# MetaFormer block: the clip finished on ScalarE and its sum with x moved from VectorE to GpSimd

## The reference

```python
x = x + conv_ref(ln_c(x), weight, gamma, beta)     # ln_c: normalise over the 64 channels
t = to_tokens(x)                                   # (32, 3136, 64)
t = t + ffn_ref(ln_t(t), ...)                      # ln_t: normalise over the 64 channels again

def conv_ref(x, weight, gamma, beta):
    y = conv3x3(sign(x), sign(weight - mean) * power_of_two)
    yn = (y - mean(y)) * rsqrt(var(y) + 1e-5) * gamma + beta   # statistics over all images and pixels
    return clip(yn, -1.0, 1.0)

def ffn_ref(x, Wr, br, W1, ..., Wo, bo):           # 8 experts, 64 -> 64 -> 64 -> 64
    w = softmax(mean(x, axis=0) @ Wr + br)         # a gate for each pixel, from the mean over the images
    h = relu(bn1(x @ W1 + b1)); h = relu(bn2(h @ W2 + b2))
    return sum over experts of w * (h @ Wo + bo)
```

## Time and profile before

| What | Value |
|---|---|
| Median of 3 runs | 1450.95 us (1448.56 to 1454.09) |
| Profiled execution | 1453.43 us, its span 1451.5 us |
| TensorE (PE) busy | 1362.0 us, 94% |
| VectorE (DVE) busy | 978.6 us, 67% |
| ScalarE (ACT) busy | 882.1 us, 61% |
| GpSimd (POOL) busy | 556.3 us, 38% |
| Mean granted TensorE clock | 0.983 of full speed |

### The profile page before, as it was taken

How to read it: one execution, slowest core, us unless ns; L and a number is a source line. 1 busy time by engine, 2 the same in 40 slices (tenths; PEclk the granted TensorE clock), 3 DMA queues, 4 the chain that set the end, 5 groups by cost and what they waited for, 6 DMA issues and landing times.

```text
span 1451.5 us, 34080 instructions
## 1 busy us (share of the span) xinstructions
PE 1362.0 (94%) x12984; PEld 661.1 (46%) x12984; DVE 978.6 (67%) x1660; ACT 882.1 (61%) x1279; POOL 556.3 (38%) x474
## 2 busy tenths in 40 slices
PE   3999974999999999999999999999999999999998
PEld 2666641444444444354444444444544444344444
DVE  5888871666667766666666666676666667666665
ACT  3666663666666666666666666666666666666643
POOL 7000052433444443344344344444334434434441
PEclk9999985999999999999999999999999999999999
DMA  9999920333233333323333323333323333332221
GB/s 160 171 159 140 132 51 26 66 71 78 46 65 70 66 72 72 64 51 68 65 72 72 78 47 65 66 70 65 78 48 65 69 65 72 72 77 46 53 46 33
DMA packets 361597, 107.08 MB, mean 74 GB/s; under 512 B 353552, under 2 KB 353776, under 8 KB 361456
## 3 DMA queue, kind: packets, MB, share of 16 engines
q1 hardware_dynamic: 360192, 103.49, 38.4%
q0 software_dynamic: 1264, 1.61, 0.6%
HBM read 78.97 MB, written 26.09 MB: 72 GB/s over the span
## 4 chain that ended last, share of the span: by engine, by line
PE 48%; issue 1%; DVE 1%; POOL 0%; ACT 0%; POOLq 0%; ACTq 0%
PE ps L549 15%; PE ps L571 15%; PE ps L587 14%; PE ps L605 2%; PE ps L638 1%; PE ps L613 1%; DVE placed L985 1%; ACT wT L776 0%; PE ps L625 0%; POOL feat L443 0%; POOL feat L446 0%; DVE o L941 0%; PE ps L632 0%; POOLq L257 0%; PE ps L642 0%
## 5 line engine op out<-in xcount | busy, mean ns | idle before, releaser
L931 DVE SCALAR_TENSOR_TENSOR v<-ps,negb,wb 128x448 f32<-128x448 f32 x896 | 570.4, 677 | 297.7 <-PE ps L571 233.8
L740 ACT ACTIVATE h<-ps,bias 128x896 f32<-128x896 f32 x448 | 451.4, 1008 | 349.8 <-PE ps L549 349.8
L549 PE MATMUL ps<-xc,w 64*64 64x448 f32 x3584 | 463.4, 541 | 14.0 <-POOL xc L434 11.0
L571 PE MATMUL ps<-h,w 64*64 64x448 f32 x3584 | 458.4, 539 | 7.4 <-issue 5.1
L587 PE MATMUL ps<-v,wo 64*64 64x448 f32 x3584 | 461.8, 542 | 3.2 <-issue 2.4
L571 PEld LDWEIGHTS ps<-h,w 64*64 64x64 f32 x3584 | 174.2, 133 | 189.0 <-issue 171.9
L549 PEld LDWEIGHTS ps<-xc,w 64*64 64x64 f32 x3584 | 163.4, 132 | 186.4 <-issue 178.9
L464 POOL TENSOR_TENSOR o<-o,upper 128x448 f32<-128x448 f32 x112 | 127.6, 1139 | 305.0 <-DVE o L941 305.0
L587 PEld LDWEIGHTS ps<-v,wo 64*64 64x64 f32 x3584 | 163.4, 133 | 174.8 <-issue 162.9
L456 POOL TENSOR_TENSOR o<-xin,gconst 128x448 f32<-128x448 f32 x112 | 129.8, 1181 | 249.3 <-ACT gconst L781 155.4
L434 POOL TENSOR_TENSOR xc<-xc,spread 128x896 f32<-128x896 f32 x56 | 122.6, 2208 | 166.4 <-DMA spread<-rs_rows 166.3
(11 more groups left out here) (151 smaller groups left out, 840.5 us busy)
## 6 DMA issues: line engine op xcount, KB each, us to landing
xa<-in_x SPq DMA_DIRECT2D x64, 392.0 KB, 6.4
xin<-in_x SPq DMA_DIRECT2D x112, 224.0 KB, 4.1
spread<-rs_rows SPq DMA_DIRECT2D x112, 224.0 KB, 4.2
out<-o SPq DMA_DIRECT2D x224, 112.0 KB, 2.5
rs_rows<-rs SPq DMA_DIRECT2D x112, 3.5 KB
rows<-in_L_ffn_g POOLq DMA_DIRECT2D x2, 256.0 KB, 6.2
rows<-in_L_ffn_v POOLq DMA_DIRECT2D x2, 256.0 KB, 6.8
cwt<-in_L_conv_weight SPq DMA_DIRECT2D x2, 144.0 KB, 2.6
```

The lines of the kernel that those rows point to most:

```text
L549: last = mm(ps[64 * two:64 * two + 64, L1_BANKS + ab, 0:NG], w1[half, P * q + C * two:P * q + C * two + C], xc[half, s, g // 2, ab ^ (g % ...
L571: last = mm(ps[64 * i:64 * i + 64, L2_BANKS[ab] + low, 0:NG], w2[rows_, Q + QUADS * i, :], h[rows_, u % 2, i, ab, :], start=True, stop=True)
L740: A(h[:, u % 2, i], ps[:, L1_BANKS:L1_BANKS + 2, 0:NG], ACT.Relu, bias=bias[:, 0, q:q + 1]).then_inc(h_done[i], 1)
L931: last = V.scalar_tensor_tensor(out=v[:, u % 2, ab, d, :].rearrange("p (b w) -> p b w", w=W), in0=ps[:, L2_BANKS[ab] + d, 0:NG].rearrange( ...
```

## The change

The second half of the clip leaves VectorE. With t = relu(SCALE * y + OFFSET1) as before, ScalarE makes a second pass over the same buffer, t = relu(2 - t), which is 2 - min(t, 2). GpSimd then forms xin - t, which is x + clip(yn) - 1, so `gconst` has a bias of +1. The first pass is now at places 6, 8, 10, 12 and the second (`over`) at 8, 10, 12, 14, ahead of the first pass of that place. The sums have no place of their own: they stand in GpSimd's queue, those of groups 0 and 1 of chunk k + 2 ahead of `norm(k+1)`, those of groups 2 and 3 behind `feature(k+1)`. `add_upper(k, 1)` moves from behind `feature` to ahead of it. Before the chunks, GpSimd forms all four sums of chunk 0 first and those of chunk 1 between `norm(0)` and `feature(0)`.

```diff
-        bn = sb("bn", [P, 17], F32)
+        bn = sb("bn", [P, 18], F32)
+        (TWO = bn[:, 17:18], set to 2.0 by V.memset)
...
         STEADY = Schedule(
-            t=(8, 10, 12, 14), x1=(13, 16, 17, 21), centre=(20, 28),
+            t=(6, 8, 10, 12), over=(8, 10, 12, 14), centre=(20, 28),
...
# GpSimd
+                def add_clip(q, s, g):
+                    if g % 2 == 0:
+                        pool.wait_ge(x_loaded[g // 2], 32 * q + 32)
+                    pool.wait_ge(t_done, G * q + g + 1)
+                    xg = xin[:, s, BG * g:BG * g + BG, :]
+                    nc.gpsimd.tensor_tensor(xg, xg, t[:, g].rearrange("p (b w) -> p b w", w=W), ALU.subtract).then_inc(x1_done, 1)
...
                     add_const(k, s, G - 1)
                     add_upper(k, 0)
+                    if left > 1:
+                        for g in range(2):
+                            add_clip(k + 2, s, g)
                     if left:
                         for p in range(STEPS):
                             norm(k + 1, 1 - s, p)
+                    add_upper(k, 1)
+                    if left:
                         feature(k + 1, 1 - s)
-                    add_upper(k, 1)
+                    if left > 1:
+                        for g in range(2, G):
+                            add_clip(k + 2, s, g)
                     add_upper(k, 2)
...
+                for g in range(G):
+                    add_clip(0, 0, g)
                 for p in range(STEPS):
                     norm(0, 0, p)
+                for g in range(G):
+                    add_clip(1, 1, g)
                 feature(0, 0)
...
# ScalarE
+                def rest_of_clip(q, g):
+                    act.wait_ge(t_low, G * q + g + 1)
+                    A(t[:, g], t[:, g], ACT.Relu, bias=TWO, scale=-1.0).then_inc(t_done, 1)
...
+                    for g in places_at(at.over, h) if at is STEADY else ():
+                        rest_of_clip(q, g)
                     for g in places_at(at.t, h):
                         act.wait_ge(x1_done, G * q + g + 1)
...
-                        A(..., yq, ACT.Relu, bias=OFFSET1, scale=SCALE).then_inc(t_done, 1)
+                        A(..., yq, ACT.Relu, bias=OFFSET1, scale=SCALE).then_inc(t_low, 1)
+                    for g in places_at(at.over, h) if at is AHEAD else ():
+                        rest_of_clip(q, g)
...
-                        A(gconst[:, s, :], ps[:, Y, 0:W], ACT.Copy, bias=-1.0).then_inc(g_done, 1)
+                        A(gconst[:, s, :], ps[:, Y, 0:W], ACT.Copy, bias=1.0).then_inc(g_done, 1)
...
# VectorE
-                    for g in places_at(at.x1, h):
-                        if g % 2 == 0:
-                            dve.wait_ge(x_loaded[g // 2], 32 * q + 32)
-                        dve.wait_ge(t_done, G * q + g + 1)
-                        xg = xin[:, s, BG * g:BG * g + BG, :]
-                        V.scalar_tensor_tensor(out=xg, in0=t[:, g].rearrange("p (b w) -> p b w", w=W), scalar=2.0, in1=xg,
-                                               op0=ALU.min, op1=ALU.add).then_inc(x1_done, 1)
```

More of the change, by code:

```diff
@@ L37, with __init__ @@
 class Schedule:
-    def __init__(self, t, x1, centre, var, root, square, inv, logits, gate, turn, wb):
-        self.t, self.x1, self.centre = t, x1, centre
+    def __init__(self, t, over, centre, var, root, square, inv, logits, gate, turn, wb):
+        self.t, self.over, self.centre = t, over, centre
         self.var, self.root, self.square, self.inv = var, root, square, inv
@@ L81, in metaformer_kernel @@
         wT = sb("wT", [C, W], F32)
-        bn = sb("bn", [P, 17], F32)
-        SCALE, OFFSET, SW, OFFSET1 = bn[:, 0:1], bn[:, 1:2], bn[:, 2:3], bn[:, 16:17]
+        bn = sb("bn", [P, 18], F32)
+        SCALE, OFFSET, SW, OFFSET1, TWO = bn[:, 0:1], bn[:, 1:2], bn[:, 2:3], bn[:, 16:17], bn[:, 17:18]
         gb = sb("gb", [P, 2], F32)
@@ L158, in metaformer_kernel @@
         x_loaded = [sem(f"x_loaded{p}") for p in range(STEPS)]
+        t_low = sem("t_low")
         t_done = sem("t_done")
@@ L217, in metaformer_kernel @@
         STEADY = Schedule(
-            t=(8, 10, 12, 14), x1=(13, 16, 17, 21), centre=(20, 28),
+            t=(6, 8, 10, 12), over=(8, 10, 12, 14), centre=(20, 28),
             var=34, root=36, square=38, inv=(40, 41), logits=58, gate=60, turn=62, wb=63)
         AHEAD = Schedule(
-            t=(0, 0, 0, 0), x1=(0, 0, 0, 0), centre=(1, 2),
+            t=(0, 0, 0, 0), over=(0, 0, 0, 0), centre=(1, 2),
             var=3, root=3, square=3, inv=(3, 3), logits=5, gate=5, turn=5, wb=5)
@@ L337, in _ @@
             def _(pool):
-                for s, n in (*((u, 1) for u in u_done), (feat_done, 1)):
+                for s, n in (*((u, 1) for u in u_done), (feat_done, 1), (x1_done, G)):
                     pool.sem_inc(s, n)
@@ L761, in prep @@
                             y[:, bass.ds(q, 1), BG * g:BG * g + BG, :].rearrange("p o b w -> p (o b) w")
-                        A(t[:, g].rearrange("p (b w) -> p b w", w=W), yq, ACT.Relu, bias=OFFSET1, scale=SCALE).then_inc(t_done, 1)
+                        A(t[:, g].rearrange("p (b w) -> p b w", w=W), yq, ACT.Relu, bias=OFFSET1, scale=SCALE).then_inc(t_low, 1)
+                    for g in places_at(at.over, h) if at is AHEAD else ():
+                        rest_of_clip(q, g)
                     if h == at.var:
@@ L810, in _ @@
                 V = nc.vector
-                for s, n in ((v_done[0], 1), (v_done[1], 1), (out_done, 1), (x1_done, G)):
+                for s, n in ((v_done[0], 1), (v_done[1], 1), (out_done, 1)):
                     dve.sem_inc(s, n)
@@ L815, in _ @@
                 V.memset(sgn[:], 0.0)
+                V.memset(TWO, 2.0)
                 V.memset(gate_w[:], 0.0)
```

## The result

The changed kernel takes 1456.96 us (median of 9 runs, 1454.91 to 1459.94) against 1450.95 us before (9 runs). The ratio is 1.0039, 95% interval 1.0023 to 1.0055. Measured once more beside the later experiments it is 1.0024 (1.0004 to 1.0043). So the change costs 0.2 to 0.5%. The forecast was 1454, no change within 0.5%.

What follows compares the result with a forecast made beforehand. TensorE was taken to set the chunk, 42.78 us each. -11 (lock) + 3.6 (ScalarE) + 5 (GpSimd) + 5.0 (prologue) = +2.6 us gave 1456.0 for the profiled execution, 1454 against the median; range 1440 to 1469.

Steps and rivals of the forecast that it cites:

- The removed pass: VectorE's L952 in the chunks: its lock waits with GpSimd no longer reach TensorE, -11 us, bounds -5 and -17.
- the 40%: Share of L952's 26.7 us excess over its time alone that was taken to reach TensorE.
- the 64% of the single case shown: At one first centring, 1.10 us of TensorE idleness for 1.71 us of L952's excess beside norm.
- The blocks between 23 and 32 us of a chunk: Sign to look for in the changed profile: TensorE slots there at 0.75 us.
- ScalarE: Second pass of 658 ns makes layer 1 start 0.14 us late behind upper and L740: +3.6 us, bounds +1.5 and +9.
- GpSimd in a chunk: Sums and logits late in the shortest chunks and those with late norm: +5 us, bounds +2 and +16.
- three chunks with a late `norm`: Chunks where the spread of rs lands late: sums 1.3 us behind the second centring, 3 x 1.3 us.
- The prologue: Before the chunks, first centring +3.55 us, then four sums ahead of feature(0) delay the logits: +5.0 us, bounds 4 and 7.
- GpSimd as the bound (2): In the chunks, the second centring waits for the fourth sum, +16 instead of +5: 1465 us; chance 0.23.
- Much more from the lock (3): 64% of lock waits reached TensorE, other costs at their low ends: -9.5 us, 1441; chance 0.2.
- No wait disappears (4): The change only moves work, lock waits give nothing back: 1461 us; chance 0.03.
- ScalarE's rival: ScalarE's second pass takes 749 ns, costing +9 us in the chunks: 1460 us; chance 0.08.

Runs made afterwards that it cites:

- the spare pass with one input: Changed kernel plus an unread VectorE sum over 448 columns, one SBUF input, at the old pass's places in 26 chunks: 1462.25 us, 1.0049 of before.
- prologue_vector: Changed kernel, but chunks 0 and 1 prepared as before, by one ScalarE pass and VectorE's min-and-add: 1454.61 us, 1.0000 of before.
- sum_left_out: Kernel before with VectorE's min-and-add pass replaced by a one-column copy: 1445.81 us, 0.9952 of before.
- replanned: Changed kernel with chunks 0 and 1 prepared as before, ScalarE passes re-placed, all sums ahead of norm, feature ahead of add_upper(k, 1): 1446.77 us, 0.9949 of before.

## Why the prediction was right

**The removed pass.** Forecast -11 us, with bounds -5 and -17. The slots say -7.8, the kernel without the pass -7.0. The mechanism was right and the 40% too high. The third pass of a chunk had 8.9 us of excess, of which 0.21 x 26 = 5.5 reached TensorE (62%, the 64% of the single case shown). The fourth had 17.7, of which about 2 came through (13%). Weighted, that is 29%: the cheap kind was two thirds of all, and I had given both the same weight. That the 0.62 us of the pass itself are worth nothing is shown by the spare pass with one input, whose chunks take the same time. The blocks between 23 and 32 us of a chunk, forecast at 0.75 us, are not: the first centring keeps 0.93 us, and 0.92 with the pass left out, so 0.18 us of the old wait never was the lock's.

**ScalarE.** Forecast 658 ns, measured 660. Forecast +3.6 us, measured +2 to +2.6 (0.08 to 0.10 us a chunk). `h` is 0.28 us late (0.32 was worked out), but layer 1 is not what waits; `upper` itself is, for layer 3 one block earlier. I had priced only the wait behind `upper`, and not looked up who waits for `upper`.

**GpSimd in a chunk.** Forecast +5 us, of which 3.9 for three chunks with a late `norm`. Measured +1.8 to +3.4, all at the logits. The case of the earlier trace rows, in the changed kernel:

```profile
709.84 4.14 POOL L435 TENSOR_TENSOR xc<-xc,spread 128x896 f32<-128x896 f32 x2 [4.80 <-DMA spread<-rs_rows]
...
718.05 1.06 PE L591 MATMUL ps<-h,w 64*64 64x448 f32 x8
719.74 0.29 PE L645 MATMUL ps<-wr,feat 64*56 64x8 f32 x5 [0.64 <-POOL feat L449]
...
721.93 0.98 PE L625 MATMUL ps<-xin,centre 64*64 64x448 f32 x8 [0.26 <-POOL xin L473]
```

The logits wait 0.94 us here beyond their usual time (0.58 before), then the sum 0.26. The other two late chunks of before were on time in this execution (chunks of 42.31 and 42.28 us), in the repeat one of them was late again (a chunk of 44.68 us, `norm` 26.8 us into it) and the other not. How late `spread` lands changes from run to run. The forecast had the right cause and took one execution's count of it for fixed.

**The prologue.** Forecast +5.0, measured +4.5 in the profile. `prologue_vector` gets back 4.0 of it in its profile, and 3.5 to 5.7 us by the ratios, 1.3 of them outside the span. The first centring was forecast for 218.7 and stands at 219.27 less the 0.54 us of the first stage. `feature(0)` behind four sums did set the logits. GpSimd's four took 4.39 us.

**The sum** came out at +2.6 against +2.5 between the two spans, with each term smaller than forecast and their errors cancelling: -7.8 + 2.1 + 1.8 + 4.5 is +0.6, and 0.5 of the first stage and 1.4 of waits without a shown cause make the rest. So the causes were right, but that 2.6 met 2.5 is luck. The timed ratios give +3.5 to +5.7. 1.3 us of that lie outside the span, where the forecast had taken the 1.9 us of before for the changed kernel too. The 2.2 to 4.4 us that are left have the profile's 2.5 among them; over the twelve profiles the end of the first stage alone moves between 208.7 and 212.9 us.

**The rivals.** GpSimd as the bound (2): out, TensorE waited 0.3 us for it in all chunks. Much more from the lock (3): out by `sum_left_out`. No wait disappears (4): out, 1.14 fell to 0.93. (The 1460 of ScalarE's rival should have been 1459: 9 us in place of 3.6 adds 5.4.) The Trainium skill's advice (GPSIMD Engine Reference, "Engine selection") to leave two-input work on VectorE is not borne out here: 1.14 us on GpSimd instead of 0.62 on VectorE is the better place, once nothing waits for it (`replanned`, 0.9949), because what VectorE's pass cost was the lock.

## What to carry to other kernels

A pass on an engine that isn't the bound costs what it makes others wait, not its duration: look for its stretched instances, and weigh each place by what stands behind it. Before work is moved, ask of each queue that it joins who waits for the neighbours (`upper`, the logits), and treat the stretch ahead of the steady loop apart, since nothing hides anything there. When a change moves the time little, time its parts: here a gain of 7 us and three costs stood in it, and all three could be planned away (0.9949 in place of 1.0039).

## What the hardware showed that I had not expected

- With TensorE 0.1 us later, the time that VectorE's third pass lost to the lock went from 8.9 to 19.0 us (the fourth's from 17.7 to 13.5): a two-input pass that begins just behind a GpSimd instruction waits for it, one that begins just ahead doesn't. GpSimd loses too: a `norm` pass takes 2.21 us on average before and 2.09 once nothing meets it.
- At least one of TensorE's waits with no shown cause recurs. In the chunk that starts at 1236.80, layer 2 follows layer 1 1.80 us late, 25 us into the chunk, and the same chunk has 0.98 to 2.08 us at that place in all eleven other profiles. What it waits for wasn't tried.
- A GpSimd sum whose two inputs are the same columns of one tile takes 0.93 us, with two tiles 1.14.
- The end of the first stage moves by up to 4.2 us over the twelve profiles (208.70 to 212.90 us), though its code differs by little more than one small memset, and by 1.3 us between the two profiles of the changed kernel (209.50 and 210.82). Single profiles of this kernel compare only stage by stage.
